# One tile of every super fetched row by row on the queues of SyncE and ScalarE, output stores moved to ScalarE, layernorm means in PSUM

## The reference, cut to what matters

```python
h = relu(layernorm(x)); h = (h @ W_node.T).reshape(N, 4, 32)
e = (edge_attr_64 @ W_edge.T).reshape(E, 4, 32)
att = sum(concat([h[src], h[dst], e], -1) * a, -1)
att = where(att > 0, att, 0.2 * att)
m   = max(segment_max(att, dst), 0)
ex  = exp(att - m[dst])
denom = segment_sum(ex, dst) + (E - deg)[:, None] * exp(-m)
out = x + segment_sum((ex / denom[dst])[:, :, None] * h[src], dst)
```

## Time and profile before

| | |
|---|---|
| median of 3 runs | 2111.48 us (2108.53 to 2115.55) |
| the profiled execution's own time | 2113.5 us |
| its span | 2111.7 us |
| busy: DVE, POOL, PE, ACT | 1565.6, 1561.5, 1473.7, 758.7 us |
| mean granted TensorE clock | 0.617 of full speed |
| indirect gathers: from x, from the table | 40, 1596 |
| row DMAs: SyncE, ScalarE | 2000, 1200 |

### The profile page before, as it was taken

The page is one execution under the profiler, slowest core; times in us unless marked ns, Lnnn a source line. Parts: engine busy times, 40 slices in busy tenths (PEclk is TensorE's granted clock), DMA queues, the critical chain, the costliest instruction groups (busy, mean ns, idle before and its releaser), DMA issues.

```text
span 2111.7 us, 44654 instructions
## 1 busy us (share of the span) xinstructions
PE 1473.7 (70%) x8347; PEld 1228.0 (58%) x8348; DVE 1565.6 (74%) x4474; ACT 758.7 (36%) x2294; POOL 1561.5 (74%) x1647
## 2 busy tenths in 40 slices
PE   7448777777677686776777777667677677666676
PEld 6436566666566575665655556555565566555554
DVE  8767867778786877867787777776776776776777
ACT  7633433334343332423433233233233333333333
POOL 7777777777777777777777777777777777777770
PEclk9755656566655655665666556665655556566556
DMA  9943343343434333333433334334333333334331
GB/s 269 306 142 108 95 112 92 93 111 98 111 96 110 96 108 96 93 110 94 113 94 101 102 95 111 92 92 110 93 92 93 111 92 109 95 93 110 91 92 30
DMA packets 128388, 229.59 MB, mean 109 GB/s; under 512 B 44167, under 2 KB 87251, under 8 KB 121427
## 3 DMA queue, kind: packets, MB, share of 16 engines
q0 software_dynamic: 52352, 110.59, 23.3%
q1 hardware_dynamic: 71703, 114.59, 16.3%
q10 hardware_dynamic: 4132, 2.69, 0.5%
HBM read 182.02 MB, written 45.70 MB: 108 GB/s over the span
## 4 chain that ended last, share of the span: by engine, by line
POOL 39%; issue 24%; DVE 12%; PE 11%; SPq 5%; ACTq 2%; DVEq 2%; ACT 2%; DMA 2%; POOLq 0%
POOL gath L628 37%; PE bank_rn L1426 6%; PE bank_w L1483 4%; SPq L337 3%; DVE vals L1019 3%; DVE bank_rn L899 2%; POOL gath L598 2%; ACTq L93 1%; DVEq L93 1%; ACTq L337 1%; DVE s_sum L975 1%; DMA resets<-ef 1%; SPq L93 1%; DVE den L1063 1%; DVE den L1067 1%
## 5 line engine op out<-in xcount | busy, mean ns | idle before, releaser
L628 POOL DMA_INDIRECT gath<-h_table,idx x1596 | 1513.4, 948 | 490.8 <-issue 482.3
L1483 PEld LDWEIGHTS bank_p<-vals,onehot 128*128 128x128 f32 x1664 | 383.2, 332 | 102.8 <-DVE vals L1019 63.5
L1483 PE MATMUL bank_p<-vals,onehot 128*128 128x137 f32 x1664 | 415.7, 443 | 12.7 <-DVE vals L1019 12.7
L1483 PEld LDWEIGHTS bank_w<-vals,onehot 128*128 128x128 f32 x1664 | 344.4, 302 | 95.5 <-DVE vals L1019 73.8
L1279 ACT ACTIVATE ab<-ab_log 128x8 f32<-128x8 f32 x209 | 43.6, 208 | 987.9 <-DVE ab_log L946 872.4
L1483 PE MATMUL bank_w<-vals,onehot 128*128 128x137 f32 x1664 | 372.2, 408 | 20.9 <-DVE vals L1019 20.4
L1459 PE MATMUL bank_s<-s_live,onehot_bits 128*128 128x24 bf16 x1672 | 79.3, 181 | 324.6 <-ACT onehot_bits L1301 306.9
L1426 PEld LDWEIGHTS bank_rn<-w_edge_bd,ef 128*128 128x128 f32 x1664 | 282.8, 268 | 19.0 <-DMA ef<-in_edges 19.0
L1426 PE MATMUL bank_rn<-w_edge_bd,ef 128*128 128x8 f32 x1664 | 278.7, 309 | 18.7 <-DMA ef<-in_edges 18.7
L911 DVE SCALAR_TENSOR_TENSOR onehot_bits<-bank_w,tables,zz 128x1024 bf16 (+1 forms) x209 | 268.3, 1284 | 27.3 <-issue 12.1
L1459 PEld LDWEIGHTS bank_s<-s_live,onehot_bits 128*128 128x128 bf16 x1672 | 74.9, 110 | 351.4 <-ACT onehot_bits L1301 347.0
(11 more groups left out here) (185 smaller groups left out, 1626.5 us busy)
## 6 DMA issues: line engine op xcount, KB each, us to landing
ef<-in_edges SPq DMA_DIRECT2D x52, 1024.0 KB
gath<-h_table SPq DMA_DIRECT2D x2000, 0.5 KB
out_x<-x_all SPq DMA_DIRECT2D x210, 128.0 KB
gath<-h_table,idx POOLq DMA_INDIRECT x1596
gath<-h_table ACTq DMA_DIRECT2D x1200, 0.5 KB
x_all<-in_x SPq DMA_DIRECT2D x14, 448.0 KB, 12.8
out_x<-x_all SPq DMA_DIRECT2D x14, 448.0 KB, 14.9
h_table<-gath SPq DMA_DIRECT2D x12, 462.0 KB
```

The costliest lines, as they stand in the source:

```text
L628: e.indirect_dma_start(gath[:, q * GPS + g, t * ROW:(t + 1) * ROW], None, table, bass.IndirectOffsetOnAxis(idx[:, q, g * TILES + t:g * TIL ...
L1483: ins = e.matmul(half_p[q], onehot[q][:, t, :], vals[q][:, t, :], start=(t == 0), stop=(t == TILES - 1))
```

## The change

- `HANDED`: every super from 3 on (49 of them) now leaves one tile to the row DMAs, where 25 did. SyncE issues 88 of the 128 rows in portions of 32, 28 and 28, ScalarE 40 in portions of 8, 8, 8 and 16 in the four steps.
- SyncE no longer walks through the steps. It has a list per super (`feed`): wait for `released`, load of indices, resets, terms and offsets, 32 rows, the wait for the edge products and the load of edges, and 28 and 28 rows for the super after next. It doesn't signal `gathered` any more.
- VectorE waits for the DMA semaphores itself (`rows_landed`). Its loop over supers is written out for four supers at a time, as those of ScalarE and GpSimd already were.
- ScalarE issues the output stores, one at the end of each step.
- `EARLY` is 6 groups (48 gathers from x) where it was 5. The room for this comes from staging one more chunk of table rows elsewhere (in `tables`), from row banks used in one fixed order, and from keeping the means (`twice_mean`) in a PSUM bank.

```diff
-EARLY = GPS + 1
+EARLY = GPS + 2
-STAGED = 2
+STAGED = 3
-HANDS = (SUPERS - HAND_FIRST + 1) // 2
+HAND_QS = (0, 1, 2, 3)
+HANDED = [b for b in range(HAND_FIRST, SUPERS) if b % RING in HAND_QS]
-SP_PARTS, ACT_PARTS = (12, 8, 12, 8), (8, 4, 8, 4)
+SP_PARTS, ACT_PARTS = (32, 28, 28), (8, 8, 8, 16)
+EDGES_AT = 1
...
+        twice_mean = bank_n[:, 512 - WINDOWS:512]
...
-        def row_bank(c, k):
-            return ((bank_p, bank_r)[c % 2], bank_s, bank_n)[k]
+        def row_bank(k):
+            return (bank_p, bank_s, bank_r)[k]
...
             def feed(i, q, last_turn):
...
+                wait(e, released, b + 2)
                 settle(e)
...
+                if to_come >= 3:
+                    next_indices(b + 3, (q + 3) % RING)
+                wait(e, scan_b, b)
+                settle(e)
+                load_resets(b)
+                if to_come:
+                    next_terms(b, q)
...
+                if to_come >= 3:
+                    next_offsets(b + 3, (q + 3) % RING)
+                for k, rows in enumerate(SP_PARTS):
+                    if k == EDGES_AT and to_come:
                         next_edges(b)
+                    if by_hand:
+                        rows_by_hand(e, d_hand_sp, next_q, sum(SP_PARTS[:k]), rows)
...
-                    by_hand = g == HAND_SLOT and q % 2 == 1 and not (
-                        isinstance(i, int) and i == 0 and q == 1)
+                    by_hand = g == HAND_SLOT and handed(i, q)
                     for t in range(1 if by_hand else 0, LAST_TILES if last else TILES):
...
-            def z_columns(b, slot0):
-                wait(e, gathered, b + 1)
+            def rows_landed(i, q, last_turn):
...
+                if handed(i, q):
+                    for sems, rows in ((d_hand_sp, SP_ROWS), (d_hand_act, ACT_ROWS)):
+                        e.wait_ge(sems[q], (hands_before(i, q) + 1) * (rows * 16))
+                        settle(e)
+                e.wait_ge(d_gath[q], i * (each * 16) + at_first * 16)
+                settle(e)
+            def z_columns(i, q, last_turn):
+                b, slot0 = i * RING + q, q * GPS
+                rows_landed(i, q, last_turn)
                 wait(e, e_mm, b * PAIR + PAIR)
...
+                    store((past_0, past_1)[q], s_1)
+            def store(w, s_1):
+                wait(e, s_ou, s_1)
+                settle(e)
+                e.dma_start(out[:, bass.ds(w, 2), :], x_all[:, bass.ds(w, 2), :]).then_inc(d_out, 16)
...
-                    if k == 0 and c > 1:
-                        wait(e, n_arow, rows_before(c - 2) + 3)
-                    if k in (3, 6) and c:
-                        wait(e, n_arow, rows_before(c - 1) + (6 if k == 3 else width(c - 1)))
+                    if k in (0, 3, 6) and c:
+                        wait(e, n_arow, rows_before(c - 1) + min(k + 3, width(c - 1)))
```

More of the change, by code:

```diff
@@ L220, in build @@
         stats = early[:, 0:WINDOWS * 6].rearrange("p (w c) -> p w c", c=6)
-        twice_mean, var, gap, rstd = (early[:, (6 + i) * WINDOWS:(7 + i) * WINDOWS] for i in range(4))
+        var, gap, rstd = (early[:, (6 + i) * WINDOWS:(7 + i) * WINDOWS] for i in range(3))
         s2_keep = tables[:, :, :].rearrange("p k c -> p (k c)")[
@@ L516, in feed @@
             def feed(i, q, last_turn):
                 b = i * RING + q
-                final = last_turn and q == RING - 1
-                def by_hand(k):
-                    if final:
-                        return
-                    tile, which = hand_tile(i, q)
-                    if k == 0 and q % 2:
-                        wait(e, released, b + 2)
-                        settle(e)
-                        e.wait_ge(d_hand_offs, tile * 16 + 16)
-                        settle(e)
-                    if k == 0 and q % 2 == 0 and not (last_turn and q == RING - 2):
-                        hand_offsets(tile + 1, 1 - which)
-                    rows_by_hand(e, d_hand_sp[which], which,
-                                 (1 - q % 2) * HALF + sum(SP_PARTS[:k]), SP_PARTS[k])
@@ L1124, in _ @@
             e.reg_mov(end_pair, next_end)
-            with e.Fori(1, SUPERS) as b:
-                wait(e, z_ready, b * 4)
-                steps(beside(b, e.snap((b % RING) * GPS, min_val=0, max_val=SLOTS - GPS)))
+            for q in range(1, RING):
+                feed(0, q, False)
+            with e.Fori(1, SUPERS // RING - 1) as i:
+                for q in range(RING):
+                    feed(i, q, False)
+            for q in range(RING):
+                feed(SUPERS // RING - 1, q, True)
             wait(e, z_ready, SUPERS * 4)
@@ L1316, in step_3 @@
                     z_maxima(b, slot0)
+                next_i, next_q = (i, q + 1) if q + 1 < RING else (i + 1, 0)
                 def by_hand(k):
[L1319 removed]
+                    if final or not handed(next_i, next_q):
                         return
[L1321 to L1323 removed]
+                    if k == 0:
+                        wait(e, released, b + 1)
                         settle(e)
[L1325 removed]
+                        e.wait_ge(d_hand_offs, (b + 1 - HAND_FIRST) * 16 + 16)
                         settle(e)
[L1327 to L1328 removed]
+                    rows_by_hand(e, d_hand_act, next_q, SP_ROWS + sum(ACT_PARTS[:k]), ACT_PARTS[k])
                 walk(nc, e, bounds, b - 1, pair,
```

196 lines of the change are left out of this document (81 added, 115 removed).

## The result

The changed kernel takes 2174.91 us (2173.80 to 2178.78, 4 runs) where the kernel before takes 2111.94: ratio 1.0294, 95% interval 1.0278 to 1.0310, 63 us slower. The forecast was 2083 us, with a range of 2071 to 2104. The profiled execution has a span of 2177.0 us at a granted clock of 0.644.

A forecast was written before the change was run, and what follows sets the result against it. GpSimd's gathers, one every 1.251 us, were taken as the bound before and after. Gathers -30.0, start of super 4 +1.6 and end -0.4 gave -28.8 us: 2111.5 to 2082.7, or 2083 us; range 2071 to 2104.

The forecast's parts named there:

- SyncE's list: SyncE's issue work per super (88 rows, offset loads, other DMAs, loop jump): 36.6 us against GpSimd's 38.8, 2.2 to spare.
- Rival 1: SyncE's issue work per super becomes the bound; with 2.0 us per load of 32, 40.3 us and 2155 us; chance 0.11.
- rival 2: The walk over supers (VectorE, TensorE, ScalarE) becomes the bound, ScalarE's rows fully exposed: 39.8 us per super, 2131 us; chance 0.05.
- Gathers, -30.0: GpSimd, from super 4 on: 24 table gathers fewer at 1.251 us each, -30.0 us.
- rival 3: GpSimd's gathers get dearer beside twice as many small DMAs, 0.018 us each eating the gain: 2111 us; chance 0.05.
- Start of super 4, +1.6 (bounds -3 to +5): GpSimd's first gather of super 4, waiting for VectorE's release of super 0, comes 1.6 us later than at 178.26 us.
- (a): Prelude: the sixth early group makes ScalarE's last row, and all that follows, 5.1 us later; bounds +3 to +8.
- (b): VectorE's first edge terms no longer wait for SyncE's next edge load and landing checks: -1.0 us.
- (c): Super 1: the wait of 3.50 us goes, but TensorE's step 2 matmuls are late next: -2.5 us.
- The end, -0.4: Last super: the signal hop goes, -0.4 us; final stores move from SyncE to ScalarE, between -0.6 and +2 us.
- The walk's pace, 35, and ScalarE's +0.5: VectorE, TensorE and ScalarE need about 35 us per super, including 0.5 charged for ScalarE's extra rows and stores.
- extreme: SyncE's offset loads grow with each number, 63 ns each: 5.6 us for 88, 39.9 us per super, 2135 us.

The follow-up runs named there:

- 80/48 split: Changed kernel with 80 rows by SyncE (28, 28, 24) and 48 by ScalarE (8, 12, 8, 20) instead of 88 and 40: 2072.08 us, ratio 0.9814.

## Why the prediction was wrong

The step that failed is *SyncE's list*, in the term "Three offset loads of 757 ns with 0.1 us around them: 2.6". Measured, they are 6.3 us: the row of before was of 8 and 12 numbers, and I took its duration for 28 and 32. The other terms of that sum held: rows 30.5 against 30.2, the five DMAs 2.8 against 2.9, the jump 0.7 against 0.86. The list is 36.6 + 3.7 = 40.3 us instead of 36.6, above GpSimd's 38.8, and the forecast's 2.2 us "to spare" were smaller than the error of one term. Rival 1 described this, at 2.0 us a load and 40.3 us a list: 2155 us. It had 0.11.

Rival 1's own price was 20 us too low, because it added only a pace to the forecast and left both ends as they were. A kernel that waits for GpSimd ends 47 us after the last gather. When SyncE is the bound, it isn't so: the last offset load starts at 2088.5 us, 28 rows stand behind it until 2099.8, the resets of super 50 are loaded only then (its scan begins at 2102.0), and two supers have still to be walked, in all 88.5 us. Against the 80/48 split, whose span is 2071.0 us, the changed kernel's 2177.0 come out like this: up to the start of the stretch 138.2 us for 168.0; the stretch itself 1950.3 (48.67 supers at 40.07 us between the first and the last of 147 loads) for 1856.5 (1484 gathers); the end 88.5 for 46.6. That is -29.8 + 93.8 + 41.9 = 105.9 us, where rival 1 had 72 on a forecast 11 us too high.

Two other prices of rivals don't come out of their own terms, and neither decided anything. Rows at 0.39 us make a list of 36.6 - 30.5 + 88 by 0.39 = 40.4 us and a time of 2160, not 41 and 2190. And rival 2, with 5.8 us exposed and nothing gained at the signal, is 37 + 5.8 = 42.8 us and 2275; its 39.8 and 2131 keep the gain of 3 us that its condition denies.

*Gathers, -30.0.* Right where nothing else binds. In the 80/48 split the first gather of super 4 starts at 168.01 us and the last at 2024.47:

```profile
168.01 0.94 POOL L578 DMA_INDIRECT gath<-h_table,idx  x1 [4.09 <-DVEq L1022]
...
2024.47 0.94 POOL L578 DMA_INDIRECT gath<-h_table,idx  x1 [0.30 <-issue]
```

(2024.47 - 168.01) / 1484 = 1.251 us, as before. That excludes rival 3: gathers didn't get dearer with every super's rows beside them.

*Start of super 4, +1.6 (bounds -3 to +5).* Missed. In the changed kernel:

```profile
169.88 0.94 POOL L578 DMA_INDIRECT gath<-h_table,idx  x1 [5.09 <-DVEq L1022]
```

169.88 - 178.26 = -8.4 us, and -10.25 in the 80/48 split. The parts can be read from ScalarE's last rows of the prelude and VectorE's first two edge terms. In the changed kernel:

```profile
82.43 0.71 ACT L1149 ACTIVATE gath<-bank_rn,zz 128x132 f32<-128x132 f32 x2
...
129.68 0.29 DVE L861 TENSOR_TENSOR z_cols<-bank_rn,gath 128x128 f32<-128x128 f32 x1 [5.58 <-PE bank_rn L1416]
...
160.91 0.28 DVE L861 TENSOR_TENSOR z_cols<-bank_rn,gath 128x128 f32<-128x128 f32 x1
```

At 80/48 with the means in SBUF, the same rows, and GpSimd's first gather of super 4:

```profile
87.46 0.71 ACT L1148 ACTIVATE gath<-bank_rn,zz 128x132 f32<-128x132 f32 x2
...
173.76 0.94 POOL L577 DMA_INDIRECT gath<-h_table,idx  x1 [0.30 <-issue]
```

(a) Forecast +5.1. ScalarE's last row ends at 83.1 us where it ended at 81.5: +1.6. With the means in SBUF it ends at 88.2, +6.7, inside my bounds of +3 to +8. So the forecast for the sixth group wasn't far off, but I had charged the means' move to PSUM at nothing, and it took 8.9 us out of the early gathers, which end near 63 us instead of 71 to 73.

(b) Forecast -1.0. From ScalarE's last row to the first edge terms it was 48.9 us and is 46.5: -2.3 (in the 80/48 split -4.4, with the means in SBUF -5.1).

(c) Forecast -2.5. From the first edge terms to the second it was 38.9 us and is 31.2: -7.7 (-7.6 in the two others). This is the largest miss of the three. The wait of 3.50 us was only part of what super 1 lost; what the rest was wasn't followed.

1.6 - 2.3 - 7.7 = -8.4 us. The bound on the other side, GpSimd itself, was off as well: it was ready at 169.88 - 5.09 = 164.8 us, ten us before my 175. With the means in SBUF it began super 4 at 173.76 us without waiting for VectorE, so nearly all of that is the early gathers again. Those 5.75 us against the 80/48 split's 168.01 are the 5.8 us that the means were worth in the experiment.

*The end, -0.4.* 46.6 us from the last gather to the end in the 80/48 split, 47.0 before: -0.5 without the rounding.

With these the sum works for the 80/48 split: -30.0 - 10.25 - 0.5 = -40.75 us on a span of 2111.7 gives 2070.95, and its span is 2071.0. The forecast's model of GpSimd was right. Had SyncE's list kept under 38.8, the time would have lain 11 us below its 2083, by the start alone, and still in the range.

*The walk's pace, 35, and ScalarE's +0.5 (rival 2).* Right. In the changed kernel the first edge terms, while the walk still had a lead to use up, are 34.8 us apart, (369.9 - 160.9) / 6:

```profile
L861 DVE TENSOR_TENSOR z_cols<-bank_rn,gath x7: 280/281/281, 160.9 to 369.9; 128x128 f32<-128x128 f32 x7
```

`live` waits for `ab` 39.4 us in all over 62 steps, less than 1 us per super. VectorE's longer loop does stop at its jump, up to 5.0 us in the row of `s_sum` "issue" above (50.3 us in 13 stops; ten of them lie four supers apart, at 4.1 to 5.0 us), as the prediction allowed.

*What a load costs by its size.* "12 numbers take no longer than 8" was the prediction's reason against rival 1, and so it is: in the kernel before the medians are 803 ns for 8 and 757 for 12. But the row was too short to show the rest. On SyncE a load of 4 took 555 ns, of 8 787, of 24 (80/48) 1682, of 28 1900 and of 32 2131. From 12 to 28 that is (1900 - 757) / 16 = 71 ns for each number, and from 28 to 32 it is 58 ns, close to the 63 ns of rival 1's "extreme". The Trainium skill, page "Runtime: NRT & Kernel Launch", section "Instruction fetch mechanics", has register loads at about 200 ns for each register even in bulk; worked out from that figure, 32 numbers would take an estimated 6.4 us. The runs agree with it that the cost grows with the number, at a third of its price. The page describes loads from HBM, and `hand_offs` lies in SBUF, so the two may not be the same case.

*What would show it.* Three of the signs that I had named as "wrong" came: offset loads over 1.5 us on SyncE, a pace above 38.8, and waits of GpSimd for `released` (the row of DVEq L1022 above: 25 of them, up to 1.6 us). Edge terms that wait for row DMAs didn't come, nor, in the main part, edge products that wait for `ef`; the wait showed at the scan instead, which I hadn't named.

## What to carry to other kernels

When work moves onto a queue that was half empty, add up that queue's list entry by entry, and give each entry whose size lies outside the trace both its bounds: here one 0.76 us row, stretched from 12 to 32 numbers, was short by 3.7 us for a slack of 2.2. A list at 94% of the bound is a reason to move a little less: eight rows of 128 on the other queue turned 65 us too many into 38 us saved, on one chip. And it may be too little slack on another, where the same split was 11% slower. And when a change looks like mere housekeeping (an operand into PSUM), look in the trace for what slows down beside the operation that reads it.

## What the runs showed of the hardware

- A load of offsets into registers on SyncE took 555 ns for 4 numbers, 787 for 8, 757 for 12, 1900 for 28 and 2131 for 32 (medians). Single plain DMAs of 528 bytes were issued every 0.334 us (32 in 10.66 us).
- A GpSimd indirect gather took 1.74 instead of 0.94 us when it began just after a VectorE `scalar_tensor_tensor` with both operands in SBUF, and 0.94 when one operand was in PSUM or when the gather had begun first; VectorE's operation took 1.08 us in both.
- The jump at the end of a loop of four supers cost SyncE 3.45 us (42.90 against 39.45) and VectorE 4.1 to 5.0.
- On two chips the same program took 2912 and 2902 us instead of 2112, with a GpSimd gather at 944 to 947 ns, a row DMA on SyncE at 0.63 us in the mean (0.335 in the median), and waits of GpSimd of up to 3.8 us that the first chip didn't show. A split of work with under 2 us of slack in 38.8 on one chip (80/48, 0.98) was 11% slower than the kernel before on such a one.
